# First layer of a four-layer graph network: GpSimd's clearings between scatters set before every second scatter in place of every sixth

## The reference, cut to what matters

```python
# layer 0: four times y <- A y, A sparse with one weight per edge
def step(y, _):
    msg = weights[:, None] * y[col]
    y_new = jax.ops.segment_sum(msg, row, num_segments=N_NODES)
    return (y_new, None)
y, _ = jax.lax.scan(step, x, None, length=LAYER_NUMBER)   # LAYER_NUMBER = 4
...
h = jnp.maximum(_layernorm(x, axis=-1), 0.0)
x = x + _L0_gnn_ref(h, edge_weight, src, dst)
```

## Time and profile before

| | us |
|---|---|
| median of 3 unprofiled runs | 16985.49 |
| lowest and highest | 16977.59, 16991.23 |
| span of the profiled execution | 19981.4 |
| PE, DVE, ACT, POOL busy in the profiled execution | 15319.5, 14525.3, 11839.5, 9064.2 |
| first layer in the profiled execution | 2792 to 11067 |

### The profile page before, as it was taken

The page is one execution under the profiler, slowest core; times in us unless marked ns, Lnnn a source line. Parts: engine busy times, 40 slices in busy tenths (PEclk is TensorE's granted clock), DMA queues, the critical chain, the costliest instruction groups (busy, mean ns, idle before and its releaser), DMA issues. The chain is left out here.

```text
span 19981.4 us, 345555 instructions
## 1 busy us (share of the span) xinstructions
PE 15319.5 (77%) x83251; PEld 13719.6 (69%) x83252; DVE 14525.3 (73%) x36440; ACT 11839.5 (59%) x23449; POOL 9064.2 (45%) x26210
## 2 busy tenths in 40 slices
PE   0158825698559966895689699978886899859997
PEld 0058813498339944794479688877775788759996
DVE  5645542397338833793369799989997899869997
ACT  2000022397228833793369577779996999947775
POOL 1368837601771077206720577624344244457730
PEclk9555555699669966896689899999998999979998
DMA  7611120000000000000000211122221222211111
GB/s 215 166 29 40 39 68 12 14 21 21 12 12 21 20 16 13 19 20 16 14 17 21 38 40 39 38 53 90 88 90 63 70 74 75 66 28 31 31 29 18
DMA packets 1232239, 892.88 MB, mean 45 GB/s; under 512 B 834722, under 2 KB 1140870, under 8 KB 1222022
## 3 DMA queue, kind: packets, MB, share of 16 engines
q1 hardware_dynamic: 868038, 738.16, 12.7%
q0 software_dynamic: 245760, 117.75, 3.0%
q10 hardware_dynamic: 118080, 33.61, 0.9%
HBM read 627.08 MB, written 261.69 MB: 44 GB/s over the span
## 5 line engine op out<-in xcount | busy, mean ns | idle before, releaser
L1548 PE MATMUL powers_sums<-powers_b_hot,powers_spread 128*128 128x224 f32 x26400 | 6315.6, 388 | 1918.4 <-issue 1666.3
L1548 PEld LDWEIGHTS powers_sums<-powers_b_hot,powers_spread 128*128 128x128 f32 x26400 | 5398.4, 207 | 2837.9 <-issue 2791.6
L1652 POOL DMA_INDIRECT filled<-powers_by_b,powers_at_start x2688 | 2610.2, 971 | 4117.2 <-DMA node_rows<-powers_by_b 2678.4
L1526 DVE TENSOR_TENSOR powers_spread<-powers_a_hot,powers_held 128x640 f32<-128x640 f32 x2640 | 2152.8, 815 | 2901.8 <-PE powers_sums L1548 1838.3
L1543 ACT ACTIVATE powers_b_hot<-powers_away,ones 128x672 f32<-128x672 f32 x2640 | 1986.1, 753 | 3508.7 <-PE powers_sums L1548 2296.0
L1537 ACT ACTIVATE powers_away<-wide,powers_minus_b 128x224 f32<-128x224 f32 x6600 | 2717.1, 472 | 117.5 <-ACT powers_minus_b L1721 40.1
L2376 PE MATMUL relate_got<-relate_hot,relate_table 112*128 112x512 f32 x10560 | 2118.8, 344 | 185.9 <-ACT relate_hot L2337 68.2
L2392 PE MATMUL relate_mixed<-relate_mix,relate_picked 128*128 128x128 f32 x13200 | 1821.5, 286 | 210.5 <-DVE relate_picked L2441 114.1
L2337 ACT ACTIVATE relate_hot<-relate_away,ones 112x1280 fp32r<-112x1280 bf16 x1320 | 1780.9, 1349 | 336.1 <-DMA conv_given<-wide_filled 232.0
L2376 PEld LDWEIGHTS relate_got<-relate_hot,relate_table 112*128 112x128 f32 x10560 | 1627.6, 194 | 446.8 <-issue 146.0
L1529 DVE TENSOR_SCALAR powers_b_hot<-wide,powers_b_val 128x224 f32<-128x224 f32 x6600 | 1896.7, 337 | 0.0
(11 more groups left out here) (479 smaller groups left out, 24846.7 us busy)
## 6 DMA issues: line engine op xcount, KB each, us to landing
relate_codes<-pair_rows SPq DMA_DIRECT2D x264, 800.0 KB
powers_given<-filled SPq DMA_DIRECT2D x528, 200.0 KB
rec<-relate_running SPq DMA_DIRECT2D x132, 400.0 KB
filled<-powers_by_b,powers_at_start POOLq DMA_INDIRECT x2688
wide_filled<-order_blanks SPq DMA_DIRECT2D x30, 1320.0 KB
conv_given<-wide_filled SPq DMA_DIRECT2D x132, 300.0 KB
relate_given<-wide_filled SPq DMA_DIRECT2D x132, 300.0 KB
grouped<-order_blanks POOLq DMA_DIRECT2D x20, 1320.0 KB
```

Source lines behind the costliest of these rows:

```text
L1526: dve.tensor_tensor(spread, a_hot.unsqueeze(3).to_broadcast([P, n, 8, D]), message.unsqueeze(2).to_broadcast([P, n, 8, D]), ALU.mult)
L1548: mm = pe.matmul(gathering.sums[:, bass.ds(group * STRIDE, WINDOW)], spread[:, j].rearrange("p a d -> p (a d)"), b_hot[:, j, :], start=Fal ...
L1652: pool.indirect_dma_start(filled, bass.IndirectOffsetOnAxis(to, 0), rows, None).then_inc(spread_out[block % 2], 16)
```

## The change

GpSimd's rest in the first layer comes before every second scatter, as in the later layers, in place of every sixth. The count that a rest waits for is worked out with the same number.

```diff
-BURST, CALM_BURST, RESTS = 6, 2, 10
+CALM_BURST, RESTS = 2, 10
...
                     for a in range(sends(block)):
                         many = sent(range(block)) + a
-                        if many % BURST == 0 and many:
-                            rest(pool, still, rested, r * ((sent(range(SPREAD_BLOCKS)) - 1) // BURST) + many // BURST, gate)
+                        if many % CALM_BURST == 0 and many:
+                            rest(pool, still, rested, r * ((sent(range(SPREAD_BLOCKS)) - 1) // CALM_BURST) + many // CALM_BURST, gate)
```

## The result

| | before | after |
|---|---|---|
| median of 4 executions, us | 16982.69 | 17704.26 |
| lowest and highest | 16977.59, 16991.23 | 17675.96, 17710.49 |
| ratio, 95% interval | | 1.0421 (1.0408 to 1.0433) |
| span of the profiled execution | 19981.4 | 17674.2 |

The change makes the kernel 4.2% slower, 722 us. The direction was forecast and the time lies in the range, but the forecast rise was 424 us. The profiled execution of the kernel after is one of its four (17675.96 us).

What follows compares the result with a forecast made beforehand. PE at full clock was taken to bound a 1315 us round; with denser rests GpSimd would: 4.9 + 1370 + 46, together 1421 us, 106 more. Four rounds add 424: 16985 + 424 = 17,409 us, range 16,940 to 17,780.

Steps and rivals of the forecast that it cites:

- a PE that waits near the end of each round: Expected in the first layer's profile after: PE waits for DVE, DVE for loads, SP for GpSimd's blocks, hundreds of us per round.
- The round before, 1315: A first-layer round of the unprofiled kernel before, taken as bound by PE at its full clock: 1315 us.
- taking the whole difference out: All 2996 us between profiled execution and unprofiled median taken from the four first-layer rounds: 2064 - 749 = 1315 us each.
- GpSimd's round, 1370: GpSimd's scatters in a first-layer round: 1172 us now, plus 198 us for 228 more rests at 0.87 us, 1370 us after.
- The tail, 46: First-layer round's end after GpSimd's scatters: 20 us from load to first pass, 19 us of passes, 7 us for emptying.
- 91 blocks feed 132 turns evenly: In a first-layer round GpSimd's pace per turn goes from 8.9 to 10.4 us, where PE needs 9.4 us.
- I give it nothing: Clearings' cost to DVE's first-layer comparisons set at zero, as means were 330 and 335 ns; the skill's rule allowed 337 us.
- The starvation belongs to the profiled execution: PE's starved issue beside the first layer's scatters was put almost wholly down to the profiled execution; unprofiled rounds PE-bound.
- a pass costs the same everywhere: A PE pass at full clock was taken as 0.189 us in all stages, 530 passes in 100 us.
- real starvation, ended by the rests: Rival 1: PE is starved in unprofiled first-layer rounds too and denser rests end it, 16,810 us; chance 0.13.
- the scatters stay hidden: Rival 2: first-layer rounds stay PE-bound if GpSimd's round is at most 1264 us, time 16,985 us; chance 0.15.
- the last edge layer's pace: Rival 3: first-layer scatters run as slowly as the last edge layer's, a round of 1574 us, 18,020 us in all.

Runs made afterwards that it cites:

- e2: The kernel before with a rest at every fourth scatter of the first layer in place of every sixth: 17073.54 us, 1.0061 of before.
- e3: The kernel after with one clearing in each rest in place of ten: 17280.02 us, 1.0185 of before.
- e10: The kernel after with its dense rests only in blocks 0 to 44, 170 per round, none in the others: 17315.75 us, 1.0215 of before.
- e1: The kernel before with no rests in the first layer's scatters: 16877.23 us, 0.9948 of before.
- e6: The kernel after with 128 turns per round in place of 132, four blank turns left out: 17515.74 us, 1.0331 of before.
- e4: The kernel before with 57 clearings in each rest in place of ten: 17505.70 us, 1.0316 of before.
- e8: The kernel before with no rests at the scatters of the first layer, convolution and messages, nor at the end gathers: 16809.17 us, 0.9917 of before.
- e9: No rests at any scatter, as in e8, and 128 turns per round in place of 132: 16679.56 us, 0.9838 of before.
- e5: The kernel before, unchanged, profiled a second time: 16948.17 us, span 16946.4 us; its trace is the one called "before".

## Why the prediction was right in sign and too small

**The mechanism is the one forecast.** The scatters became the round's bound and PE ended up waiting for DVE, DVE for SP's loads, SP for the blocks: SP's wait of 1212.9 us a round, PE's passes at 422 to 479 in 100 us against "some 460", the profiled span 30 us from the median, where "within 200" was said. e2, e3 and after lie on one line, a round of G + 122 to 124 us. Only the place is off: "a PE that waits near the end of each round" stops from its first 200 passes on, and e10 shows that early stops are not made up.

**The terms, against 106 us forecast and 180.4 measured per round.**
- *The round before, 1315*: 1332.0, which takes 17 us off the loss. The step "taking the whole difference out" gave it, with PE alone as the bound. A rest before every sixth scatter is not wholly hidden: without any, the round is 1313.5, close to my 1315. Part of these 18.5 us (22 by the medians) is that PE's first pass of a round comes 9 us later in before than in e1 (49.6 us of idle time against 40.9), and DVE's comparisons take 9.5 us a round more; the two may overlap, and the rest is not split.
- *GpSimd's round, 1370*: 1390.3, 20 us more. The step is the rest's 0.87 us from one row: (1390.3 - 1170.9)/228 = 0.96.
- *The tail, 46*: 117, 71 us more, the largest miss. The step that failed is "91 blocks feed 132 turns evenly". They feed 126, and six blank turns, 57 us of PE, stand behind the last block in every round; e6 showed four of them. The other 14 us of the tail are not split. The trace of before hid it, since PE there stood half a round behind the last block for another reason; the edges per group, 18 turns at most of the 132/7, would have told it.
- In sum, 106 - 17 + 20 + 71 = 180 us a round.

**"I give it nothing"** for the clearings' load on DVE was wrong in the rows, though not in the sum. The two means of the earlier trace rows come from one stretch without GpSimd and from another kernel part; over the same part with and without rests the mean goes from 336 to 353 ns. In after the lengthening falls mostly into time in which DVE waits for loads anyway. Of the 337 us that the Trainium skill's rule allowed, 71.5 us came as longer comparisons (2014.5 against 1943.0): in after most comparisons meet no burst, and the 1493 that do take 0.40 us in the mean in place of 0.34. Beside the long bursts of e4 the rows bear the rule out, and the prediction's "the two means disagree with it" drew too much from means.

**The starvation belongs to the profiled execution**: right for the sum, wrong as a cause. It was one rare execution, and profiling as such does not bring it: the spans of after and of the eleven experiments lie within 31 us of their kernels' medians. Leaving out the rests did not bring it either in the 12 executions of e1, e8 and e9, though for so rare a thing that is weak evidence. What does is open. One reading beside it was too wide: "a pass costs the same everywhere" holds for this layer (0.189 us); the last edge layer has 1011 passes in 150 us, 0.148 us each. The sum uses only the first.

**The rivals.** 1 (real starvation, ended by the rests; 16,810) fell with e1 and e5. 2 (the scatters stay hidden) fell: G was 1390 us. Its corner was put at 1264; it lies at some 1190, mostly because of the longer tail. 3 (the last edge layer's pace, 18,020) fell: the mean scatter in after is 982 ns:

```profile
L1652 POOL DMA_INDIRECT filled<-powers_by_b,powers_at_start x672 | 660.1, 982 | 513.1 <-POOL powers_still L1494 267.9 <-issue 125.1 <-DMA node_rows<-powers_by_b 120.1
```

## What to carry to other kernels

A producer that runs ahead is free only until its own round plus the consumer's work behind its last item reaches the consumer's round; compute both from the trace, and read the second term from the last item to the end, since padding can stand there. Where slack is spent matters: against no rests at all (e1), 170 of them cost 109 us a round in its first half, and 172 cost 42 in its second. If a profiled span lies far above the times of the other executions, take a second profile before building a mechanism on the first.

## What the runs showed of the hardware

- After a pause of 4 us and more PE's next passes are slower. In before 200 take 38.09 us; the first 200 after a round's start take 40.88 and 40.70 us, and in after 300 behind a pause of 6.82 us take 59.58, where 1.5 x 38.09 is 57.1. The granted clock, whose two levels are 1.2 and 2.4 GHz, has a mean of 0.93 of the upper one over the round against 0.98, and PE's busy time for the same passes 1310.6 against 1267.2 us. Where GpSimd sets the pace, as here, PE waits for the next loads all the same.
- A stop of GpSimd for its own semaphore costs half a microsecond: 0.81 us idle before the next scatter in place of 0.30, behind one clearing (e3) as behind ten (after). The whole rest costs 0.65 us with one clearing and 0.94 with ten, so the stop is dearer than the clearings.
- A burst of one-column clearings on GpSimd holds up a DVE comparison (`tensor_scalar`, 128x224, f32) that meets it: up to 2.0 us in place of 0.33 beside 57 clearings (e4). Over the layer that is 8 ns of DVE per clearing in bursts of ten and 19 ns in bursts of 57.
